# Causal attention on one core: queries and keys in fp32 from SBUF on four 32-partition groups, heads in pairs, with a rewritten opening

## The chip, the cores and the metric

The program runs on one core of one Trainium2 chip. The metric is the device time of one execution in microseconds (us). A smaller time is better.

## What is computed

Four residual steps on x of shape 4 x 512 x 256 (2048 tokens, 16 heads of 16), of which the change touches the first:

```python
x = x + L0_xattn(layernorm(x), ctx_1024)      # causal, relative bias
x = x + L0_ffn(layernorm(x))                  # top 2 of 8 experts, gelu
x = x + L1_xattn(layernorm(x), ctx_1024)      # masked
x = x + L1_ffn(layernorm(x))                  # quantised gate, up, down

# L0_xattn, per batch b and head h (q from x; k and v from ctx_1024)
QEr  = q @ Er.T                               # 512 x 512
Srel = skew(QEr)                              # row i shifted left by 511 - i
attn = softmax(where(causal, (q @ k.T + Srel) / sqrt(16), -inf))
out  = attn @ v
```

## The kernel before

**Stages.** The program is one chain of stages: an opening (the K, V and Q projections of the first layer and its LayerNorm), the causal attention, routing and experts, the masked attention, the closing ffn. The causal attention works through 4 x 16 = 64 heads of a batch, one after the other.

**Opening (`opening`).** SP loads weights, the whole of ctxT (2 MB), the whole of x (2 MB), and the rest. PE makes keys and values half a batch at a time (`PieceProjection.product`, `ValueProjection.product`). ACT copies each 128x512 result twice (fp32, and bf16 as the first piece; L212), DVE splits off two more bf16 pieces (L222, L225, L227) and SP stores them to `packed` in DRAM, 24 transfers for the keys and 24 for the queries (L239). DVE's LayerNorm statistics run in between. The normalising itself is one call for all 16 token tiles, after the last projection of the keys, and PE's transposes (L157) and query projections (L198) wait for that. A head's queries and keys lie in DRAM as six groups of 16 rows, so that one bf16 matmul of 96 rows sums six products of pieces.

**Causal attention (`causal_attention`, L471 to L652).** Only the lower triangle is computed. It is packed in three units a head (CAUSAL_UNITS): the 128 queries of row block 3 with 512 keys; blocks 2 and 0 with 384 and 128; block 1 with 256. A head is 1280 columns (REL_W). `run_heads` runs every engine through steps n. In step n:

- SP loads the queries and keys of head n+8 from `packed` (L400), starts the skewed read of head n+4's relative scores (L515), and the write of head n+6's (L520). The skew is made by writing `stage` to `rel` in DRAM and reading it back with another row pitch, into `bias`.
- PE takes unit by unit: `score` of head n+2 (L541, bf16, and a matmul that adds the mask, L544) into psS, `turn_probs` of head n (four, four and two 128x128 transposes, L555) into psT, `relative` of head n+6 (L533) into psE. At the end of the step comes one `weigh` (L444): the probabilities of four heads by their values, as four fp32 matmuls in four column groups of 32. Each of psE, psS and psT has two banks, used in turn, so that a unit waits for the reader of the unit before the last.
- DVE adds bias and takes the row maximum in one instruction (L603, unit by unit), copies psT to PT (L611) and makes nm = -max/4 (L616). Every four heads it divides by the sums (L464, L466).
- ACT copies psE to `stage` (L643), which has two buffers, so it waits until the write of the head before the last has landed. Between the copies it does head n+1's exponentials in place, with bias nm (L648).
- Pool spreads the values of four heads (L430).

## Time and profile before

| | |
|---|---|
| median of 3 runs | 1235.87 us (1233.3 to 1241.53) |
| the profiled execution | 1240.44 us, span 1238.3 us |
| mean granted clock of TensorE | 0.929 of full speed |
| busy in the span | PE 1011.7, DVE 698.7, ACT 649.7, Pool 199.1 us |
| opening, 0 to 82.1 us | 82.1 us |
| causal attention, 82.1 to 394.2 us | 312.1 us |
| everything behind it | 844.1 us |

The span runs from the first recorded instruction to the last. 2.1 us of the execution lie outside it. The stages are divided by barriers, so their times add up. PE's busy time includes weight loads and moves that other work could cover, so it says nothing of a bound by itself.

### The profile page before, as it was taken

What the parts mean: (1) busy time and instruction counts of PE and PEld (TensorE: products, weight loads), DVE (VectorE), ACT (ScalarE), POOL (GpSimd) and SP (SyncE); (2) the same over time, 40 slices, a digit from 0 to 9 for tenths busy, and PEclk for the clock granted to TensorE, in tenths of its full rate; (3) what the DMA queues carried; (4) which work ended last, traced back from release to release, by engine and by line L of the source; (5) the groups of instructions that cost most, each with busy time, mean ns of one, the idle gap of its engine ahead of it and who ended that gap; (6) DMA issues with size and microseconds to landing.
All of it is one profiled execution on the core that took longest, in us unless ns stands there. A gap on an engine that the chain in (4) does not pass through costs nothing. (4 is left out here: it accounts for less than half of the span.)

```text
span 1238.3 us, 22330 instructions
## 1 busy us (share of the span) xinstructions
PE 1011.7 (82%) x6466; PEld 632.3 (51%) x6467; DVE 698.7 (56%) x2148; ACT 649.7 (52%) x1354; POOL 199.1 (16%) x466
## 2 busy tenths in 40 slices
PE   5746778877888769899999993538999999987487
PEld 3413455444454559898899993212333333334344
DVE  3844778888887541121111110866766666683697
ACT  1345767777773423222233331425777777763687
POOL 0000000000000012233222210002222222240232
PEclk9876999999999979899999997668999999998699
DMA  7478989999983845666666662463111111110001
GB/s 234 149 261 317 332 326 341 342 341 339 339 335 108 315 136 202 220 212 216 215 216 228 221 218 77 131 207 106 46 46 46 48 45 45 46 31 9 1 30 39
DMA packets 91721, 220.29 MB, mean 178 GB/s; under 512 B 8854, under 2 KB 52214, under 8 KB 85654
## 3 DMA queue, kind: packets, MB, share of 16 engines
q1 hardware_dynamic: 87926, 209.46, 49.2%
q0 software_dynamic: 3744, 10.23, 2.2%
q8 instruction: 22, 0.36, 0.1%
q14 instruction: 29, 0.24, 0.1%
HBM read 143.14 MB, written 76.41 MB: 177 GB/s over the span
## 5 line engine op out<-in xcount | busy, mean ns | idle before, releaser
L775 DVE CUSTOM_DVE_ANT_0 unused<-mpsS,mask_bias 128x512 bf16<-128x512 f32 x256 | 172.0, 691 | 84.0 <-PE mpsS L708 83.8
L1482 ACT ACTIVATE hT<-ph,w 128x128 f32<-128x128 f32 x312 | 89.0, 368 | 208.8 <-PE ph L1456 208.8
L802 ACT ACTIVATE mPT<-mpsB 128x512 f32<-128x512 f32 x256 | 152.6, 597 | 81.2 <-PE mpsB L715 74.8
L1456 PE MATMUL ph<-xT,w 128*128 128x128 f32 x1248 | 151.5, 281 | 8.8 <-DMA w<-in_w1p 8.1
L1501 DVE TENSOR_TENSOR xn<-py,b 128x256 f32<-128x256 f32 x39 | 16.5, 424 | 248.7 <-PE py L1466 248.7
L555 PE MATMUL psT<-ident,scores 128*128 128x128 f32 x640 | 108.0, 285 | 57.2 <-ACT scores L648 55.3
L1456 PEld LDWEIGHTS ph<-xT,w 128*128 128x128 f32 x1248 | 146.9, 197 | 11.9 <-issue 10.9
L603 DVE CUSTOM_DVE_ANT_0 scores<-psS,bias 128x512 f32<-128x512 f32 (+3 forms) x256 | 119.7, 487 | 47.8 <-DMA bias<-rel 21.8
L643 ACT COPY stage<-psE 128x512 f32<-128x512 f32 (+1 forms) x192 | 97.5, 510 | 93.6 <-DMA rel<-stage 58.1
L1466 PE MATMUL py<-w,hT 128*128 x624 | 141.2, 379 | 0.7 <-DVE xn L1501 0.7
L648 ACT ACTIVATE scores<-scores,nm 128x128 f32<-128x128 f32 (+3 forms) x256 | 136.6, 565 | 5.2 <-DVE nm L616 5.2
L611 DVE COPY PT<-psT 128x512 f32<-128x512 f32 (+1 forms) x192 | 114.6, 599 | 18.1 <-PE psT L555 17.7
L1466 PEld LDWEIGHTS py<-w,hT 128*128 128x128 f32 x624 | 115.6, 190 | 15.2 <-issue 1.1
L708 PE MATMUL mpsS<-mqk 96*128 96x512 bf16 x256 | 101.2, 397 | 18.7 <-DMA mqk<-packed 14.4
L555 PEld LDWEIGHTS psT<-ident,scores 128*128 128x128 f32 x640 | 68.9, 145 | 80.8 <-ACT scores L648 59.4
L713 PE MATMUL mpsB<-mqk 99*128 99x512 bf16 x256 | 99.0, 387 | 0.1
L715 PE MATMUL mpsB<-maskT,identb 128*128 128x512 bf16 x256 | 98.6, 385 | 0.0
L533 PE MATMUL psE<-ErP,qk 96*128 96x512 bf16 (+3 forms) x256 | 70.8, 322 | 21.1 <-DMA qk<-packed 16.2
L1430 POOL DMA_INDIRECT pair_out<-xn,dst_row x39 | 42.4, 1087 | 214.6 <-DVE xn L1501 214.6
L541 PE MATMUL psS<-qk 96*128 96x512 bf16 (+3 forms) x256 | 73.4, 312 | 1.2 <-DVE mx L603 1.2
L430 POOL TENSOR_TENSOR spreada<-V,zerosa 128x272 f32<-128x272 f32 x16 | 11.5, 719 | 364.7 <-PE psOa L444 281.7
L444 PE MATMUL psOm<-mPT,spreadm 128*32 128x512 f32 x512 | 67.8, 604 | 0.8 <-ACT headsm L451 0.8
(258 smaller groups left out, 1435.8 us busy)
## 6 DMA issues: line engine op xcount, KB each, us to landing
rel<-stage SPq DMA_DIRECT2D x64, 640.0 KB, 6.6
bias<-rel SPq DMA_DIRECT2D x64, 640.0 KB, 7.2
w<-in_w1p SPq DMA_DIRECT2D x39, 1028.0 KB, 5.7
qk<-packed SPq DMA_DIRECT2D x64, 192.0 KB
mqk<-packed SPq DMA_DIRECT2D x64, 192.0 KB
w<-in_w2p SPq DMA_DIRECT2D x8, 1024.0 KB
b<-in_b SPq DMA_DIRECT2D x39, 128.0 KB, 6.1
got<-pair_out SPq DMA_DIRECT2D x8, 512.0 KB, 8.3
```

Source lines behind the costliest of these rows:

```text
L555: tr = nc.tensor.transpose(psT[bank][:, to:to + P], scores[slot][:, at:at + P], ident[:, :])
L603: ttr = nc.vector.tensor_tensor_reduce(out=scores[slot][:, at:at + w], in0=psS[(NU * slot + u) % 2][:, off:off + w], in1=bias[slot][:, at: ...
L611: nc.vector.tensor_copy(PT[r][:, 512 * u:512 * u + WU[u]], psT[(NU * slot + u) % 2][:, 0:WU[u]]).then_inc(s_tev, 1)
L643: nc.scalar.copy(stage[slot % 2][:, 512 * i:512 * i + WU[i]], psE[(NU * slot + i) % 2][:, 0:WU[i]]).then_inc(s_eev, 1)
L648: ex = nc.scalar.activation(scores[slot][:, at:at + w], scores[slot][:, at:at + w], ACT.Exp, bias=nm[:, slot, i:i + 1], scale=1.0 / 4)
L708: nc.tensor.matmul(psS[i % 2][:, :], qk[slot][0:KP, i * P:(i + 1) * P], qk[slot][0:KP, S:2 * S], start=True, stop=True).then_inc(s_smm, 1)
L713: nc.tensor.matmul(psB[i % 2][:, :], qk[slot][:, S + i * P:S + (i + 1) * P], qk[slot][:, 0:S], start=True, stop=False)
L715: nc.tensor.matmul(psB[i % 2][:, :], identb[:, :], maskT[:, i, :], start=False, stop=True).then_inc(s_bmm, 1)
L775: nc.vector.tensor_tensor_reduce(out=unused[:, i, :], in0=psS[i % 2][:, :], in1=mask_bias[:, i, :], scale=1.0, scalar=-3.0e38, op0=ALU.add ...
L802: nc.scalar.activation(PT[r][:, j, :], psB[j % 2][:, :], ACT.Exp, scale=1.0 / 4).then_inc(s_exp, 1)
L1456: mm = nc.tensor.matmul(ph[half][:, q * P:(q + 1) * P], w1[i][:, dk * F + f * P:dk * F + (f + 1) * P], xT[i][:, dk, :], start=(dk == 0), s ...
L1466: mm = nc.tensor.matmul(py[:, 0:D], hT[i][:, f, :], w2[:, bass.ds(e, 1), f * D:(f + 1) * D].rearrange("p a d -> p (a d)"), start=(f == 0), ...
```

## The change

- `packed` is no longer used by this attention. The projections leave fp32 keys in xnT (`kf`) and fp32 queries in the memory of xn (`qf`). The host permutes the heads' rows in the weights, so that heads 0 to 3 of a group of eight lie in the first 16 partitions of the four 32-partition groups and heads 4 to 7 in the second 16. An even-numbered four (`odd` = 0) uses 16 rows. An odd four uses all 32 rows of its group, with queries from ctxT whose other 16 rows DVE has zeroed (`odd` mask, one 128x512 product per batch and half). `er` is Er on all eight 16-row places.
- Heads go in pairs. Pair p lies in row groups 0 and 1 (p even) or 2 and 3 (p odd). In step n PE issues, unit by unit, the scores of pair n+2, the relative scores of pair n+5 (the other two row groups), the mask matmuls (`hide`), and the transposes of pair n. psE, psS and psT are one two-bank tensor each, a bank per head, so that a unit waits for the reader of the unit before it. ACT's psE copies and DVE's psT copies take both heads in one instruction. A step has two `weigh` calls.
- The third `bias` pair lies in x's memory. SP reloads ctxT (2 MB) and x (2 MB) when the last score has been read.
- In the opening, ctxT and x come by batch, LayerNorm runs per batch between the value copies, ACT copies a projection once, and nothing is split or stored.

```diff
+                stage = [sb(ctx, f"stage{r}", [P, 2, REL_W]) for r in range(2)]
+                bias = [sb(ctx, f"bias{r}", [P, 2, REL_W]) for r in range(2)]
+                bias.append(x[:, :, :].rearrange("p t d -> p (t d)")[:, 0:2 * REL_W].rearrange("p (a w) -> p a w", a=2))
...
+                def pair_at(n, ahead):
+                    return n + ahead if 0 <= n + ahead < NP else None
+
+                def piece(p, u, h):
+                    return (NU * p + u) * 2 + h
+
+                def where(p, h):
+                    m = 2 * p + h
+                    b, eh, odd, r = m // HEADS, m % HEADS // ROUND, m % ROUND // GROUP, m % GROUP
+                    return b, eh, odd, slice(ROWS * r, ROWS * r + (ROWS if odd else DH))
+
+                def query(p, h, i):
+                    b, eh, odd, rows = where(p, h)
+                    if odd:
+                        return ctxT[rows, eh, b * S + i * P:b * S + (i + 1) * P]
+                    return qf[rows, b, eh, i * P:(i + 1) * P]
+
...
+                    def read(p):
+                        for h in range(2):
+                            slot = (2 * p + h) % ROUND
+                            sp.wait_ge(s_wr[slot], 16 * (2 * p // ROUND + 1))
...
+                            if p >= len(bias):
+                                sp.wait_ge(s_soft, piece(p - len(bias), NU - 1, h) + 1)
                             skewed = bass.AP(rel[slot].ap().tensor, P - 1, [[REL_W - 1, P], [1, REL_W]])
-                            sp.dma_start(bias[slot][:, :], skewed).then_inc(s_rd[slot], 16)
-                        if h := stage_of(n, r, it, REL):
-                            m, slot, turn = h
...
+                            sp.dma_start(bias[p % len(bias)][:, h, :], skewed).then_inc(s_rd[slot], 16)
+
+                    def write(p):
+                        sp.wait_ge(s_eev, NU * (p + 1))
+                        for h in range(2):
+                            slot = (2 * p + h) % ROUND
+                            wait(sp, s_rd[slot], 16 * (2 * p // ROUND))
+                            sp.dma_start(rel[slot][:, :], stage[p % 2][:, h, :]).then_inc(s_wr[slot], 16)
+
+                    for n in range(-REL, NP - SOFT):
+                        if (p := pair_at(n, READ)) is not None:
+                            read(p)
+                        if (p := pair_at(n, REL)) is not None:
+                            write(p)
+                    for i, name in enumerate(("L1_WkT", "L1_WvT")):
+                        sp.dma_start(wkv[:, i, :, :], a[name].rearrange("(k p) e -> p k e", p=P)).then_inc(s_wkv, 16)
+                    sp.wait_ge(s_soft, 2 * NU * NP)
+                    for half in range(2):
+                        part = slice(half * TOK // 2, (half + 1) * TOK // 2)
+                        sp.dma_start(ctxT[:, :, part], a["ctxT"].rearrange("(k p) t -> p k t", p=P)[:, :, part]).then_inc(s_back, 16)
+                    sp.dma_start(x[:, :, :], a["x"].rearrange("b (i p) d -> p (b i) d", p=P)).then_inc(s_back, 16)
+                    sp.wait_ge(s_wkv, 32)
+                    sp.wait_ge(s_back, 48)
...
+                    def relative(p, u):
...
+                            rows = where(p, h)[3]
+                            for i, off, w in units[u]:
+                                mm = nc.tensor.matmul(psE[:, h, off:off + w], query(p, h, i), er[rows, S - w:S],
+                                                      start=True, stop=True)
                         mm.then_inc(s_emm, 1)
...
+                    def score(p, u):
+                        for h in range(2):
+                            wait(pe, s_soft, piece(p, u, h) - 1)
+                            for at, (i, off, w) in enumerate(units[u]):
+                                nc.tensor.matmul(psS[:, h, off:off + w], query(p, h, i), key(p, h, w),
+                                                 start=(at == 0), stop=False)
+
+                    def hide(p, u):
+                        for h in range(2):
+                            for at, (i, off, w) in enumerate(units[u]):
+                                mm = nc.tensor.matmul(psS[:, h, off + w - P:off + w], identb[:, :], dmask[:, :],
+                                                      start=False, stop=(at == len(units[u]) - 1))
+                            mm.then_inc(s_smm, 1)
+
+                    def turn_probs(p, u):
+                        for h in range(2):
+                            if u == 0:
...
+                            for j, off, w in CAUSAL_KEYS[u]:
+                                for i in range(j, NI):
+                                    at = place[i][0] + j * P
+                                    to = off + (i - j) * P
+                                    tr = nc.tensor.transpose(psT[:, h, to:to + P], scores[p % 3][:, h, at:at + P], ident[:, :])
...
+                    for n in range(-REL, last + 1):
+                        early, soft, late = (pair_at(n, k) for k in (REL, SOFT, 0))
                         for u in range(NU):
-                            if soft:
-                                score(soft[0], soft[1], qk[(r + SOFT) % ROUND], u)
-                            if late:
...
+                            if soft is not None:
+                                score(soft, u)
+                            if early is not None:
+                                relative(early, u)
+                            if soft is not None:
+                                hide(soft, u)
+                            if late is not None:
+                                turn_probs(late, u)
+                        g, half = divmod(n - 2, 2)
+                        if 0 <= g < NBH // GROUP:
+                            for j in (2 * half, 2 * half + 1):
+                                at, w = key_place[j]
+                                vals.weigh(pe, g, g % 2, j, s_tev, NU * 2 * (g + 1),
+                                           lambda h: PT[(2 * g + h // 2) % 4][:, h % 2, at:at + w])
+                        if n % 2 == 0 and 0 <= n // 2 - 2 < NBH // GROUP:
+                            vals.turn(pe, n // 2 - 2, 0)
...
+                                    continue
+                                m = 2 * soft + h
+                                if u == 0:
+                                    dve.wait_ge(s_rd[m % ROUND], 16 * (m // ROUND + 1))
+                                    if soft >= 3:
+                                        dve.wait_ge(s_tmm, NU * (soft - 2))
+                                dve.wait_ge(s_smm, piece(soft, u, h) + 1)
...
+                            if late is not None:
+                                dve.wait_ge(s_tmm, NU * late + u + 1)
+                                nc.vector.tensor_copy(PT[late % 4][:, :, 512 * u:512 * u + WU[u]],
+                                                      psT[:, :, 0:WU[u]]).then_inc(s_tev, 1)
+                            if u == 0 and n % 2 == 1 and 0 <= n // 2 - 2 < NBH // GROUP:
+                                vals.divide(dve, n // 2 - 2, n // 2 % 2)
...
+                        by_row = lambda name: a[name].rearrange("(k p) e -> p k e", p=P)
+                        sp.dma_start(wk[:, :, :], by_row("L0_WkT")).then_inc(s_wk, 16)
+                        for b in range(B):
+                            cols = slice(b * S, (b + 1) * S)
+                            sp.dma_start(ctxT[:, :, cols], a["ctxT"].rearrange("(k p) t -> p k t", p=P)[:, :, cols]).then_inc(s_cx[b], 16)
+                            if b == 0:
+                                sp.dma_start(wv[:, :, :], by_row("L0_WvT")).then_inc(s_wv, 16)
+                                sp.dma_start(bk[:, :], a["L0_bk"]).then_inc(s_wk, 16)
+                                sp.dma_start(bv[:, :], bass.AP(a["L0_bv"].tensor, 0, [[0, P], [1, D]])).then_inc(s_wv, 16)
+                        for b in range(B):
+                            sp.dma_start(x[:, b * NI:(b + 1) * NI, :], a["x"][b].rearrange("(i p) d -> p i d", p=P)).then_inc(s_xb[b], 16)
                         sp.dma_start(ident[:, :], a["ident"]).then_inc(s_const, 16)
-                        q.load(sp)
...
                         ln.turn(pe, 0)
                         for b in range(B):
                             if b + 1 < B:
                                 ln.turn(pe, b + 1)
                             pe.wait_ge(ln.s_ev, DK * (b + 1))
                             for eh in range(DK):
-                                q.product(pe, DK * b + eh)
+                                queries(DK * b + eh)
 
...
+                        for b in range(B):
+                            for t in range(b * NI, (b + 1) * NI):
+                                dve.wait_ge(s_vm, t + 1)
+                                nc.vector.tensor_tensor(V[:, b * HEADS:(b + 1) * HEADS, t % NI, 0:DH],
+                                                        psV[t % 2][:, 0:D].rearrange("p (h d) -> p h d", d=DH),
+                                                        bv[:, :].rearrange("p (h d) -> p h d", d=DH), ALU.add).then_inc(s_vev, 1)
+                                if t % NI == 0:
+                                    dve.wait_ge(s_xb[b], 16)
                                 ln.stats(dve, t)
-                        ln.norm(dve, 0)
-                        dve.wait_ge(s_above, 16)
+                            ln.norm(dve, b)
...
+                        for g in range(B * DK):
+                            b, eh = divmod(g, DK)
+                            dve.wait_ge(s_qev, g + 1)
+                            nc.vector.tensor_scalar(ctxT[:, eh, b * S:(b + 1) * S], qf[:, b, eh, :], odd[:, 0:1], None,
+                                                    ALU.mult).then_inc(s_odd, 1)
```

PE in the middle of the causal attention, before: the step of one head, with `psS` the scores and masks (L541, L544), `psT` the transposed probabilities (L555), `psE` the relative scores (L533).

```order
L541 MATMUL psS<-qk 128x512
L544 MATMUL psS<-dmask,identb 128x128
L555 MATMUL psT<-ident,scores 128x128 x4
L533 MATMUL psE<-ErP,qk 128x512
L541 MATMUL psS<-qk 128x384
L544 MATMUL psS<-dmask,identb 128x128
L541 MATMUL psS<-qk 128x128
L544 MATMUL psS<-dmask,identb 128x128
L555 MATMUL psT<-ident,scores 128x128 x4
L533 MATMUL psE<-ErP,qk 128x384
L533 MATMUL psE<-ErP,qk 128x128
```

After: the first part of the step of one pair, with the scores at L532, relative scores at L524, masks at L538 and transposes at L552.

```order
L532 MATMUL psS<-xnT,ctxT 128x512 x2
L524 MATMUL psE<-er,xn 128x512 x2
L538 MATMUL psS<-dmask,identb 128x128 x2
L552 MATMUL psT<-ident,scores 128x128 x8
L532 MATMUL psS<-xnT,ctxT 128x384
L532 MATMUL psS<-xnT,ctxT 128x128
L532 MATMUL psS<-xnT,ctxT 128x384
L532 MATMUL psS<-xnT,ctxT 128x128
L524 MATMUL psE<-er,xn 128x384
L524 MATMUL psE<-er,xn 128x128
L524 MATMUL psE<-er,xn 128x384
L524 MATMUL psE<-er,xn 128x128
```

Scores and relative scores of two heads now stand directly behind each other, with both heads' masks behind them. Before, a mask and four transposes stood between a score and a relative score.

SP at the start of the causal attention, before: loads of heads (L400), writes (L520) and skewed reads (L515).

```order
L520 DMA rel<-stage 128x1280
L400 DMA qk<-packed 96x1x1024
L520 DMA rel<-stage 128x1280
L400 DMA qk<-packed 96x1x1024
L515 DMA bias<-rel 128x1280
L520 DMA rel<-stage 128x1280
```

After: the same queue, with writes at L500 and reads at L493, two at a time.

```order
L500 DMA rel<-stage 128x1280 x2
L493 DMA bias<-rel 128x1280 x2
L500 DMA rel<-stage 128x1280 x2
L493 DMA bias<-rel 128x1280 x2
L500 DMA rel<-stage 128x1280 x2
L493 DMA x<-rel 128x1280 x2
```

The loads of heads are gone from SP. Each read of a pair now stands directly behind the write of the same pair.

## Rows read from the trace of the kernel before

**Rows 1.** Windows by stage: start:end, length, busy us (instructions) per engine, clock, DMA share, GB/s.

```profile
0.00:82.10 82.10, 51.39 (x160) 29.63 (x161) 49.79 (x126) 27.20 (x43) 0.20 (x4) 0.90 0.67 221
82.10:99.20 17.10, 7.64 (x25) 2.62 (x25) 1.00 (x3) 5.78 (x12) 1.43 (x2) 0.50 0.64 213
99.20:383.30 284.10, 224.87 (x1885) 138.48 (x1884) 230.25 (x787) 205.28 (x447) 10.08 (x14) 0.96 0.89 329
383.30:394.20 10.90, 7.70 (x79) 4.22 (x77) 5.59 (x16) 3.09 (x6) 0.00 (x0) 1.00 0.00 0
394.20:1238.30 844.10, 720.06 (x4322) 457.31 (x4322) 412.09 (x1219) 408.33 (x846) 187.36 (x446) 0.93 0.38 124
```

**Rows 2.** Timeline of PE in the opening: start, length, line, operation, idle before and releaser.

```profile
12.11 3.54 PE L198 MATMUL prpsak<-ctxT,wak 128*128 128x512 f32 x4 [12.11 <-DMA ctxT<-in_ctxT]
...
20.67 3.10 PE L268 MATMUL pvpsa<-wva,ctxT 128*128 128x256 f32 x8 [1.58 <-DVE V L278]
...
44.65 1.99 PE L268 MATMUL pvpsa<-wva,ctxT 128*128 128x256 f32 x8 [0.16 <-DVE V L278]
53.24 3.50 PE L157 MATMUL lnpsa<-ident,xn 128*128 128x128 f32 x16 [6.60 <-DVE xn L131]
...
65.19 7.03 PE L198 MATMUL prpsaq<-xnT,waq 128*128 128x512 f32 x16
86.57 1.03 PE L533 MATMUL psE<-ErP,qk 96*128 96x512 bf16 x3 [14.35 <-DMA qk<-packed]
```

**Rows 3.** Timeline of SP's queue in the opening.

```profile
61.70 17.73 SPq L239 DMA_DIRECT2D packed<-piecesaq  x24
82.09 2.84 SPq L400 DMA_DIRECT2D qk<-packed  x3
```

**Rows 4.** Waits, 200 to 320 us: total us, times, longest.

```profile
ACT stage L643 <- DMA rel<-stage: 30.5, 26, 1.3
...
PE psT L555 <- ACT scores L648: 23.4, 27, 1.4
```

**Rows 5.** DMA, 200 to 320 us: packets, MB, share; then issues, median us to landing.

```profile
q1 hardware_dynamic: 10550, 40.79, 91.0%
...
rel<-stage SPq DMA_DIRECT2D x27, 640.0 KB, 6.7
bias<-rel SPq DMA_DIRECT2D x27, 640.0 KB, 7.2
```

**Rows 6.** Timeline of SP's queue after the last load of a head.

```profile
360.44 0.33 SPq L520 DMA_DIRECT2D rel<-stage  x1
...
364.79 0.32 SPq L520 DMA_DIRECT2D rel<-stage  x1
```

**Rows 7.** Timeline of DVE near the stage's end, with no transfers left.

```profile
373.69 0.69 DVE L603 CUSTOM_DVE_ANT_0 scores<-psS,bias 128x512 f32<-128x512 f32 x1
...
374.30 0.69 DVE L611 COPY PT<-psT 128x512 f32<-128x512 f32 x1
374.90 0.55 DVE L603 CUSTOM_DVE_ANT_0 scores<-psS,bias 128x384 f32<-128x384 f32 x1
...
376.94 0.69 DVE L603 CUSTOM_DVE_ANT_0 scores<-psS,bias 128x512 f32<-128x512 f32 x1
```

**Rows 8.** Timeline of PE around one `weigh`.

```profile
239.60 1.07 PE L444 MATMUL psOa<-PT,spreada 128*32 128x512 f32 x8
240.60 0.39 PE L541 MATMUL psS<-qk 96*128 96x512 bf16 x1
240.83 0.22 PE L544 MATMUL psS<-dmask,identb 128*128 128x128 bf16 x1
```

**Rows 9.** Window of 0.05 us inside that `weigh`, instructions on psOa alone.

```profile
239.65:239.70 0.05, 0.05 (x4) 0.05 (x8) 0.00 (x0) 1.00 0.75 307
```

**Rows 10.** Timeline of PE and DVE: four transposes and their copy.

```profile
241.64 0.66 PE L555 MATMUL psT<-ident,scores 128*128 128x128 f32 x4 [0.59 <-ACT scores L648]
...
242.33 0.69 DVE L611 COPY PT<-psT 128x512 f32<-128x512 f32 x1 [0.23 <-PE psT L555]
```

More of the change, by code:

```diff
@@ L82, in build @@
         s_const = sem("s_const")
-        s_ctx = [sem(f"s_ctx{i}") for i in range(2)]
         class LayerNorm:
@@ L537, in score @@
-                    def score(m, slot, q_k, u):
-                        bank = (NU * slot + u) % 2
-                        wait(pe, s_soft, NU * m + u - 1)
-                        for i, off, w in units[u]:
-                            nc.tensor.matmul(psS[bank][:, off:off + w], q_k[:, i * P:(i + 1) * P],
-                                             q_k[:, S:S + w], start=True, stop=False)
-                            mm = nc.tensor.matmul(psS[bank][:, off + w - P:off + w], identb[:, :], dmask[:, :],
-                                                  start=False, stop=True)
-                        mm.then_inc(s_smm, 1)
@@ L868, in _, with keys @@
-                        pe.wait_ge(s_const, 32)
+                        def keys(g):
+                            b, eh = divmod(g, DK)
+                            wait(pe, s_kev, g - 1)
+                            for dk in range(DK):
+                                mm = nc.tensor.matmul(psK[g % 2][:, :], wk[:, dk, eh * P:(eh + 1) * P], ctxT[:, dk, b * S:(b + 1) * S],
+                                                      start=(dk == 0), stop=(dk == DK - 1))
+                            mm.then_inc(s_km, 1)
@@ new lines, in values, with queries @@
+                        def values(t):
+                            wait(pe, s_vev, t - 1)
+                            for dk in range(DK):
+                                mm = nc.tensor.matmul(psV[t % 2][:, 0:D], ctxT[:, dk, t * P:(t + 1) * P], wv[:, dk, :],
+                                                      start=(dk == 0), stop=(dk == DK - 1))
+                            mm.then_inc(s_vm, 1)
+                        def queries(g):
+                            b, eh = divmod(g, DK)
+                            wait(pe, s_qev, g - 1)
+                            for dk in range(DK):
+                                mm = nc.tensor.matmul(psK[g % 2][:, :], wq[:, dk, eh * P:(eh + 1) * P], xnb[b % 2][:, dk, :],
+                                                      start=(dk == 0), stop=(dk == DK - 1))
+                            mm.then_inc(s_qm, 1)
```

337 lines of the change are left out of this document (121 added, 216 removed).

## The prediction

> **What bounds the kernel now.** I read the windows by stage first [rows 1]. The opening takes 82.1 us, the causal attention 312.1, the rest 844.1. The diff leaves the rest alone, so it enters the sum unchanged.
>
> The opening is a chain on PE with three gaps. PE starts at 12.11, when the first half of ctxT has landed behind 1.8 MB of queue. It idles 6.60 us before 53.24, because the normalising waits for the last key projection [rows 2]. And after its last query product (65.19 + 7.03 = 72.2) it idles 14.35 us, until a head has been stored and loaded again [rows 2]. SP's queue shows the reason: the query stores are issued until 79.4 and the loads start at 82.09 [rows 3].
>
> In the causal attention a head takes 4.35 to 4.48 us (284.1 us for 63.8 heads; two writes are 4.35 apart in [rows 6]). Two things end together there. ACT waits 26 times for the write of `stage`, 30.5 us in all, and PE waits 27 times for the exponentials, 23.4 us [rows 4]. DMA is at 91% [rows 5]. DVE alone would need 3.25 us: with no transfers left, 373.69 to 376.94 is one head [rows 7].
>
> **Part 1: the opening.** By the shapes, 1.0 MB (weights and one batch of ctxT) are ahead of the keys' first product, instead of 1.8 (weights, biases and half of ctxT): PE starts at about 7.5. It then took 34.5 us for keys and values (12.11 to 46.6 [rows 2]), of which about 3.5 us were half clock and one 1.58-us wait. The new order has its own wait, since the statistics of a batch need x, which comes behind all of ctxT. I take 31, so 38.5. Normalising lies between the value copies: for a batch DVE has about 5.5 us of work against PE's 7.3. The 6.60-us gap is gone. Transposes and queries took 53.24 to 72.2, 19.0 us, 1.5 of it at half clock; I take 18, so 56.5. One ACT copy, one DVE product and the barrier follow: **58**. The stores (24 + 24) and their wait are gone, and so is DVE's splitting. Its bounds are 54 and 63. Against 82.1 that is -24.
>
> **Part 2: the load of heads.** 192 KB of 1472 KB per head leave the queues [rows 5]. What does that give? The writes of the last heads have no such loads beside them, and are still 4.35 us apart [rows 6]. So nothing by itself.
>
> **Part 3: the matmuls.** A bf16 score of 512 columns occupied PE for 0.23 us (240.60 to 240.83 [rows 8]). An fp32 matmul of 512 columns takes two passes: 16 records in 7.03 us are 8 matmuls of 0.86 us [rows 2]. One pair has 4 x 1280 columns of scores and relative scores, 8.6 us of PE if nothing runs side by side, and it has only about 8.9 us per pair. So everything hangs on how the row groups run together. The trace has no row groups. Its nearest row is `weigh`: four fp32 matmuls of 512 columns in four column groups, eight records, 1.00 us from 239.60 to 240.60 [rows 8], where four in a row would be 3.44. In 0.05 us at 239.65 four of them run at once [rows 9]. I take 0.90 for four of 512 columns (and for a unit of 384 + 128), 0.48 for four of 256. The other end is 3.44 (one by one).
>
> A rule of the Trainium skill gives another value. "TensorE: Matmul & The Clock Gate", Part 3 (packing small matmuls), reports 3.07 times for four row groups of 32 rows with 512 columns. By it the four would take 3.44 / 3.07 = 1.12, which adds 0.22 twice and 0.12 once per pair, 17 us in all: 1232 instead of 1215. No row here shows row groups.
>
> **Part 4: the new chain.** Each of psE, psS and psT now has one buffer, so PE fills psS only after DVE has read it. Per pair: after DVE's last read of a unit come release 0.13, weight load 0.10, the four matmuls, leaving their mode 0.10, masks 0.06, and latency 0.19 (four transposes at 241.64 were seen by DVE at 242.33, 0.69 for 0.46 of work [rows 10]). That is 0.58 plus the matmuls. DVE's reads of a pair's unit are 2 x 0.61, 2 x 0.69 and 2 x 0.34 [rows 7].
>
> - unit 0 to 1: 1.24 + 1.48 = 2.72
> - unit 1 to 2: 1.40 + 1.06 = 2.46
> - unit 2 to 0 of the next pair: 0.68 + 1.48 + 1.5 = 3.66. The 1.5 are two `weigh` calls (1.79 or 0.95; mean 1.37 from [rows 8] scaled to the columns) and a turn, which now stand ahead of the next scores
> - DVE's divide: 0.16
>
> That makes 9.0 us. DVE's copies (2 x 512 in one, 1.14) lie in the gaps, its busy time is about 6.6. DMA needs 4 x 640 KB at 340 GB/s = 7.7 us, hidden. Two heads took 8.9 before. I take **8.97**: the gain in writes and loads goes into a chain with single buffers.
>
> And ACT's wait for `stage` [rows 4]? A buffer holds a pair and is filled again two pairs later, 17.9 us. Copies of a pair (3 of up to 1024 columns, 3.3) and the landing of two writes (6.7 and 1.9 for the second) fill 11.9 of them. So this wait goes, and the chain above is what is late instead.
>
> **Part 5: both ends.** To the first read of scores: four us of relative scores and copies at half clock, a landed write (6.7), a landed read (7.2) [rows 5], a score: 19, between 15 and 24. It took 17.1 before with 4.5 of load in it. Then 31 periods, 278. Behind them the last pair's reads (4), then the reload of 4.2 MB at the 329 GB/s of [rows 1], 12.8, with 1.5 of latency beside the last exponentials, transposes and divide: 18.5, between 15 and 23. The two weight loads for the second attention stay at nothing: they hide under the same tail.
>
> **Sum.** 58 + 19 + 278 + 18.5 + 844.1 = 1217.6 for the span, with 2.1 outside it 1219.7. The profiled execution was 1240.44 against a median of 1235.87. In proportion: **1215 us**. A measurement of this kernel can tell about 1% (12 us) from no change; 1% faster is 1223.5.
>
> **Rivals.**
>
> - *DMA sets the pace.* A read waits for the write issued just ahead. If each landing then stands behind the other pair's transfers, a period is 4 x 640 KB at 340 GB/s (7.7) plus 1.7 of fixed latency: 9.4, +14 us: 1230. For it: 91% share [rows 5], and the waits of [rows 4]. Against it: 13% of the bytes are gone. Chance 0.13.
> - *Row groups don't run together* (slower). The mechanism: matmuls start in the order of the program, and a second one of the same row group (the 128-column block behind the 384-column one, or the second pass of the same matmul) holds up all behind it. If only the second matmul does so, unit 1 alone suffers: 4 x 0.65 instead of 0.90 + 0.2, +1.5 a pair, +47 us: 1262. If the second pass does so too, four matmuls take five passes of 0.43, 2.15 instead of 0.90, and unit 1 more: +2.8 a pair, +87: 1302. With no overlap at all, about +5 a pair: 1370. It decides against the change from +0.8 us a pair. Against it: the eight records of `weigh` take 1.00 us, not 5 x 0.43 [rows 8], and four run at once [rows 9]. For it: those are column groups with one matmul each. Chance 0.25 (0.12, 0.08, 0.05).
> - *PE's steps are hidden* (faster still). If matmuls start as soon as psS's first bank is free and `weigh` runs beside them, DVE (6.6) or DMA (7.7) sets the pace. A period of 7.6 is -42 us: 1173. For it: PE waited 23.4 of 120 us [rows 4]. Against it: the order of the program on PE. Chance 0.13.
> - *The opening gains nothing*, because x comes too late for the statistics and PE waits there: 1237. Chance 0.02. 2.1 MB of x had landed by 20.67 [rows 2], where the wait for it ended, with less ahead of it now.
>
> The Trainium skill has the order as a rule, in the section named above: matmuls start and end in the order of the program. By it the first case of the second rival holds, and the time is 1262.
>
> **How the numbers follow.** Forecast 0.47: its own range is 1199 to 1232 (opening -4 to +5, the two ends -7 to +9, the period -0.3 to +0.3, not all together). Of it 0.36 are faster by over 1%, 0.10 within, 0.01 slower. DMA: 0.02, 0.09, 0.02. Row groups: 0.00, 0.02, 0.23. Hidden steps: 0.13 faster. Opening: 0.01 within, 0.01 slower. Together 0.51, 0.22, 0.27. The range leaves out the fastest of the hidden case (0.08) and the full hold-up and no overlap (0.12): 1180 to 1275.
>
> **What would show it.** The opening: PE's first product at 7.5, its last near 56, no idle over 2 us. Part 3: four records of psS and psE starting together, 0.9 us per unit 0. Part 4: writes on SP 9.0 apart; DVE waiting for PE's masks (L538) in every unit and hardly for `bias`. The first rival: DVE waits for `bias`, DMA share above 0.9. The second: unit 1's eight matmuls take over 2 us. What makes me wrong: any value of the four matmuls other than 0.90, since it counts three times in each of 31 pairs, or a fill that holds the next pairs up.

## The result and the profile after

The changed kernel takes 1248.24 us (median, 1238.62 to 1262.75) against 1234.96 for the kernel before: a ratio of 1.010, 95% interval 1.0078 to 1.0121. It is 1% slower, where 2% faster was forecast. The ratio leaves out one of its 20 executions, the one at 1262.75. The profiled execution took 1249.16 us, its span is 1247.4.

The windows by stage answer to [rows 1]. The stages are the opening, the way to the first scores, from there to the last scores, the end of the attention, and the rest.

```profile
0.00:55.90 55.90, 46.88 (x160) 28.22 (x161) 26.17 (x98) 18.11 (x30) 0.20 (x4) 1.00 0.30 99
55.90:83.50 27.60, 18.29 (x58) 7.75 (x58) 1.49 (x5) 8.36 (x11) 1.44 (x2) 0.55 0.60 216
83.50:384.20 300.70, 285.28 (x2310) 167.46 (x2314) 210.55 (x658) 197.22 (x349) 9.38 (x13) 0.93 0.74 262
384.20:407.50 23.30, 14.47 (x133) 8.23 (x133) 9.08 (x16) 5.38 (x11) 0.73 (x1) 0.91 0.53 181
407.50:1247.40 839.90, 719.97 (x4322) 458.34 (x4322) 412.22 (x1219) 408.76 (x846) 187.36 (x446) 0.93 0.38 125
```

| us | before | forecast | measured |
|---|---|---|---|
| opening | 82.1 | 58 | 55.9 |
| to the first scores | 17.1 | 19 | 27.6 |
| 31 pairs, and the last one's reads | 295 with the end | 278 + 4 | 300.7 |
| end | (in the line above) | 14.5 | 23.3 |
| rest | 844.1 | 844.1 | 839.9 |

The opening gave 26.2 us. The attention took 351.6 instead of 312.1, which is 39.5 more. The timeline of PE in the opening and at the start of the attention answers to [rows 2]:

```profile
7.27 3.63 PE L856 MATMUL psKa<-ctxT,wka 128*128 128x512 f32 x4 [7.27 <-DMA bka<-in_L_bk]
...
36.56 1.04 PE L156 MATMUL lnpsa<-ident,xn 128*128 128x128 f32 x8
...
48.38 7.03 PE L871 MATMUL psKa<-xnb,wqa 128*128 128x512 f32 x16
56.99 1.13 PE L524 MATMUL psE<-er,xn 16*128 16x512 f32 x4 [1.57 <-PEq L813]
59.22 2.08 PE L524 MATMUL psE<-er,xn 16*128 16x384 f32 x8 [1.10 <-ACT stage L634]
```

PE starts at 7.27, runs without a gap to the transposes at 36.56 and ends at 55.4. Behind that, PE waits for ACT's copy after every unit of relative scores. A unit's matmuls, then their copy, then the next unit's matmuls: that is the single psE. The three pairs ahead of the first scores take 7.3, 8.3 and 8.4 us (from 56.99, 64.33 and 72.63). The clock in that stretch is near 0.5.

The waits and the DMA view from 200 to 320 us answer to [rows 4] and [rows 5]:

```profile
DVE scores L596 <- PE psS L538: 32.5, 19, 2.9
ACT stage L634 <- PE psE L524: 32.2, 26, 3.2
...
PE psT L552 <- DVE PT L603: 2.8, 13, 0.2
```

```profile
q1 hardware_dynamic: 7406, 33.71, 79.4%
...
rel<-stage SPq DMA_DIRECT2D x26, 640.0 KB, 4.1
bias<-rel SPq DMA_DIRECT2D x18, 640.0 KB, 4.6
```

The wait for the write of `stage` is gone, as is PE's wait for the exponentials. DVE and ACT both wait for PE now. PE itself is busy 115.10 of the 120 us in this stretch. DVE waits for the masks 19 times in about 13 pairs: once a pair ahead of unit 0, and now and then ahead of unit 1, not in every unit as forecast. How long is a pair? The timeline of DVE gives it by the first read of each pair:

```profile
204.50 0.69 DVE L596 CUSTOM_DVE_ANT_0 scores<-psS,bias 128x512 f32<-128x512 f32 x1 [2.94 <-PE psS L538]
...
213.13 0.69 DVE L596 CUSTOM_DVE_ANT_0 scores<-psS,x 128x512 f32<-128x512 f32 x1 [1.54 <-PE psS L538]
...
223.13 0.69 DVE L596 CUSTOM_DVE_ANT_0 scores<-psS,bias 128x512 f32<-128x512 f32 x1 [2.94 <-PE psS L538]
```

Pairs take 8.63 and 10.00 us in turn, 9.32 on average. Two heads took 8.9 before. The timeline of PE in one of the long pairs says what fills it:

```profile
211.51 0.70 PE L532 MATMUL psS<-xnT,ctxT 32*128 32x512 f32 x2
211.52 0.70 PE L524 MATMUL psE<-er,xn 16*128 16x512 f32 x2
212.04 0.59 PE L532 MATMUL psS<-xnT,ctxT 32*128 32x512 f32 x2
212.06 0.59 PE L524 MATMUL psE<-er,xn 16*128 16x512 f32 x2
212.58 0.28 PE L538 MATMUL psS<-dmask,identb 128*128 128x128 bf16 x2
...
213.89 1.20 PE L532 MATMUL psS<-xnT,ctxT 32*128 32x384 f32 x3
214.51 0.60 PE L524 MATMUL psE<-er,xn 16*128 16x384 f32 x2
...
215.59 0.40 PE L538 MATMUL psS<-dmask,identb 128*128 128x128 bf16 x4
...
218.72 0.66 PE L552 MATMUL psT<-ident,scores 128*128 128x128 f32 x4 [0.21 <-DVE PT L603]
219.31 1.71 PE L404 MATMUL psOa<-PT,spreada 128*32 128x512 f32 x16
220.95 0.66 PE L417 MATMUL psXa<-ident,headsa 128*128 128x128 f32 x4
221.54 0.70 PE L532 MATMUL psS<-xnT,ctxT 32*128 32x512 f32 x2
```

In unit 0 all four matmuls start within 0.02 us and take 1.07 us to the masks (four in a row would be 3.44). So the row groups do run together. In unit 1 the first head's score starts at 213.89, and the second's with the relative scores 0.62 later, when DVE has read the second head of unit 0. The record of 1.20 us at 213.89 covers that wait, where the matmuls of one head alone are records of about 0.6. So PE's busy time holds waits of this kind. At the end of a pair, `weigh` and the turn take 2.2 us (219.31 to 221.54) on the path to the next scores.

One more thing stands out at the end of the middle stage. The last two pairs take 10.74 and 13.51 us, though PE has no relative scores left for them. The windows of this trace, and of e9 below, which runs the same instructions on PE, show it:

```profile
358.90:375.60 16.70, 16.58 (x82) 8.59 (x80) 8.63 (x27) 6.41 (x14) 0.71 (x1) 0.50 0.14 53
```

```profile
358.00:374.00 16.00, 15.18 (x108) 8.31 (x106) 11.08 (x38) 7.85 (x17) 0.72 (x1) 1.00 0.36 133
```

In the changed kernel's trace the granted clock falls to 0.50 at 358.9 and stays there until 375.6. PE was busy 7.78 of the 8 us before the fall, with no wait for a transfer. In e9 the clock stays at 1.00 and these two pairs take 8.62 and 9.95. The fall costs this execution 5.7 us. What brings it about is open.

### The profile page after: what moved, and what is told of

The parts are those of the page before. It is cut to its first block and busy times, and to the rows that moved or that the text cites. A ratio compares the mean times of both kernels' runs of the same rounds, so it can differ in the third digit from the quotient of the medians.

```text
span 1247.4 us, 21976 instructions
## 1 busy us (share of the span) xinstructions
PE 1084.9 (87%) x6978; PEld 670.0 (54%) x6979; DVE 659.5 (53%) x1993; ACT 637.8 (51%) x1245; POOL 199.1 (16%) x466
## 5 line engine op out<-in xcount | busy, mean ns | idle before, releaser
L634 ACT COPY stage<-psE 128x1024 f32<-128x1024 f32 (+1 forms) x96 | 83.6, 871 | 93.1 <-PE psE L524 90.3
L641 ACT ACTIVATE scores<-scores,nm 128x512 f32<-128x512 f32 (+3 forms) x256 | 125.2, 554 | 7.9 <-DVE nm L609 7.9
L596 DVE CUSTOM_DVE_ANT_0 scores<-psS,bias 128x512 f32<-128x512 f32 (+3 forms) x176 | 77.7, 487 | 88.4 <-PE psS L538 88.1
L603 DVE COPY PT<-psT 128x1024 f32<-128x1024 f32 (+1 forms) x96 | 100.2, 1044 | 9.7 <-PE psT L552 9.6
L552 PE MATMUL psT<-ident,scores 128*128 128x128 f32 x640 | 91.9, 285 | 11.5 <-DVE PT L603 11.3
L552 PEld LDWEIGHTS psT<-ident,scores 128*128 128x128 f32 x640 | 71.5, 145 | 17.9 <-DVE PT L603 17.5
L532 PE MATMUL psS<-xnT,xn 16*128 16x128 f32 (+3 forms) x256 | 73.2, 507 | 6.3 <-DVE mx L596 3.8
L532 PE MATMUL psS<-xnT,ctxT 32*128 32x512 f32 (+3 forms) x256 | 70.1, 496 | 3.1 <-DVE mx L596 0.6
L699 PEld LDWEIGHTS mpsS<-mqk 96*128 96x128 bf16 x256 | 24.9, 98 | 85.9 <-DVE mmx L766 35.2
```

The costliest lines, as they stand in the source:

```text
L532: nc.tensor.matmul(psS[:, h, off:off + w], query(p, h, i), key(p, h, w), start=(at == 0), stop=False)
L552: tr = nc.tensor.transpose(psT[:, h, to:to + P], scores[p % 3][:, h, at:at + P], ident[:, :])
L603: nc.vector.tensor_copy(PT[late % 4][:, :, 512 * u:512 * u + WU[u]], psT[:, :, 0:WU[u]]).then_inc(s_tev, 1)
L641: ex = nc.scalar.activation(to, to, ACT.Exp, bias=nm[:, soft % 3, h, i:i + 1], scale=1.0 / 4)
L699: nc.tensor.matmul(psS[i % 2][:, :], qk[slot][0:KP, i * P:(i + 1) * P], qk[slot][0:KP, S:2 * S], start=True, stop=True).then_inc(s_smm, 1)
```

## The experiments

Theory A at the start: PE's chain in program order sets the period, and both ends of the attention cost what single buffers at half clock cost. The rivals were that PE's order leaves time to win, that fp32 is what costs, or that transfers do.

**e1_relfirst**

```diff
-                            if soft is not None:
-                                score(soft, u)
                             if early is not None:
                                 relative(early, u)
                             if soft is not None:
+                                score(soft, u)
                                 hide(soft, u)
```

> In each unit PE issues the relative scores of pair n+5 ahead of the scores of pair n+2; nothing else is changed. Theory A (the period of 9.3 us per pair is PE's chain in program order, and in units 1 and 2 the relative scores stand 0.6 us behind a score that waits for DVE's read of the second head): the relative scores start beside the first head's, masks end 0.2 us earlier in units 1 and 2, so 8.9 us per pair and about 1236 us. Rival B (PE is simply full: 115 of 120 us busy between 200 and 320 us): the period stays within 0.1 of 9.32 and the time at 1245 to 1250.

1250.06 us, ratio to before 1.010 (1.007 to 1.014), the changed kernel's. The undisturbed pairs take 8.63 and 9.97. So the relative scores behind a waiting score cost nothing, and this part of theory A fell. The size is rival B's, its reason isn't shown: PE's records hold waits, and e3 puts the same instructions into 8.2 us a pair. In this trace the wait for the write of `stage` is back for a while (ACT waits 15.4 us for it between 200 and 320 us), and three pairs of 11.6 to 13.2 us stand among the others.

**e2_apart**

```diff
                             if soft is not None:
                                 score(soft, u)
+                                hide(soft, u)
                             if early is not None:
                                 relative(early, u)
-                            if soft is not None:
-                                hide(soft, u)
```

> Scores, masks, then the relative scores: the masks stand between them, so never more than two row groups run together, but DVE gets its scores sooner. If four groups at once are worth what their records say (1.07 us for four of 512 columns, where two times two would be 2 x 0.9), PE has 1.7 us more per pair and the period goes to about 10.5 to 11, 1285 to 1300 us. Rival: DVE's wait for the scores is the chain and PE has room, the period falls to about 8.8, 1232 us.

1296.06 us, ratio 1.047 (1.043 to 1.051). Pairs take 9.74 and 11.11 in turn, 10.43 on average, which is 1.1 more than with four groups at once. Windows of this kernel show a second loss:

```profile
104.00:154.00 50.00, 50.00 (x198) 26.55 (x196) 19.81 (x60) 18.73 (x33) 0.00 (x0) 0.52 0.49 176
154.00:200.00 46.00, 46.00 (x344) 25.89 (x344) 30.72 (x90) 28.41 (x50) 1.44 (x2) 1.00 0.71 252
```

PE is busy all the time from 104 to 154 us, and the granted clock stays at about half. The three pairs there take 16.4 to 17.9 us.

**e3_weighmid**

```diff
+                            if 0 <= g < NBH // GROUP and u < 2:
+                                for j in (2 * half + u,):
...
+                                    vals.weigh(pe, g, g % 2, j, s_tev, NU * 2 * (g + 1),
...
-                        if 0 <= g < NBH // GROUP:
-                            for j in (2 * half, 2 * half + 1):
```

> The two products of values (weigh) of a step go behind units 0 and 1 instead of both behind unit 2; the turn stays. Theory A (PE's chain has no idle place in units 0 and 1 either): the period stays at 9.2 to 9.4, 1245 to 1250 us. Rival C (weigh lies on the path only because it stands ahead of the next pair's first scores): up to 1.3 us less per pair, 8.0, about 1208 us.

1247.54 us, ratio 1.010 (1.007 to 1.012): the total says that nothing happened. The trace says otherwise. (It is of the fastest of eight executions, 1239.09.) Up to 186 us most pairs take 8.39 and 8.01 in turn, 1.1 less than before the edit: rival C. From there on they take 8 to 12.6. The waits from 186 to 320 us, and the windows, show why:

```profile
ACT stage L634 <- DMA rel<-stage: 40.4, 14, 4.4
```

```profile
110.00:186.00 76.00, 73.70 (x699) 44.78 (x698) 62.53 (x193) 59.24 (x106) 2.88 (x4) 1.00 0.85 295
186.00:320.00 134.00, 126.53 (x1077) 76.71 (x1075) 94.50 (x288) 88.10 (x158) 5.04 (x7) 0.95 0.84 267
```

The wait for `stage` is back, and where PE was held up by it the clock fell (0.68 from 228 to 232). SP's queue has the place:

```profile
126.70 0.80 SPq L500 DMA_DIRECT2D rel<-stage  x2
130.53 1.84 SPq L493 DMA_DIRECT2D bias<-rel  x2
...
176.93 1.87 SPq L493 DMA_DIRECT2D bias<-rel  x2
178.90 1.89 SPq L500 DMA_DIRECT2D rel<-stage  x2
186.63 1.86 SPq L493 DMA_DIRECT2D bias<-rel  x2
188.59 0.87 SPq L500 DMA_DIRECT2D rel<-stage  x2
```

The reads wait for the landing of their own pair's write, and the next write stands behind them. Landing, issue of two reads, issue of two writes, landing: from 176.93 to 186.63 this is 9.7 us. At 126.70 it wasn't so: the write had a gap of over 2 us ahead of it, and the reads could be issued 3.8 us later. With the faster pairs the write comes ever closer behind the reads (151.02 to 156.98 is 6.0, 168.91 to 176.93 is 8.0 us). It then lands later, by the DMA view from 200 to 320 us:

```profile
rel<-stage SPq DMA_DIRECT2D x24, 640.0 KB, 8.4
```

In the changed kernel's view it was 4.1 us.

**e4_bf16**

```diff
-            kf = xnT
+            kf = xnT[:, :, 0:TOK // 2].bitcast(BF16)
+            qodd = ctxT[:, :, 0:TOK // 2].bitcast(BF16)
...
+                        nc.vector.tensor_copy(erb[:, :], er[:, :]).then_inc(s_cc, 1)
```

> Keys, queries and Er are rounded to one bf16 piece, so that each score or relative score is one bf16 pass instead of an fp32 matmul; rows, groups, order and waits stay. This leaves out the exactness of fp32. Theory A (what PE pays for fp32 sets the period and half of the fill): 3 us of matmuls per pair become about 1, the period goes to DVE's or DMA's 7.0 to 7.7, the fill of 27.8 us to about 20, the time to about 1185. Rival D (single buffers and waits for transfers set it): the period stays above 8.8, over 1225 us.

1255.73 us, ratio 1.015 (1.012 to 1.018): slower still, though each score is one bf16 pass now (0.39 us as a record for 512 columns, where fp32 has two of 0.59 to 0.70). Pairs take 7.3 to 13.2 us, 10.1 on average. The first scores come at 72.27. Between 200 and 320 us ACT waits for the write of `stage`, and the clock is low:

```profile
ACT stage L635 <- DMA rel<-stage: 37.7, 12, 4.7
```

```profile
200.00:320.00 120.00, 94.49 (x745) 51.36 (x744) 81.66 (x253) 75.89 (x139) 4.34 (x6) 0.84 0.83 263
```

Rival D by the numbers. So theory E was formed: the order on SP's queue makes a chain of landings of 9 us and more once a write is issued right behind the reads. In the changed kernel's trace the chain isn't closed: between 200 and 320 us SP waits 48.5 us for ACT's copies ahead of the writes, 3.8 us a pair. So the loop of landing and issue needs only some 5.5 us there, as long as reads and writes don't overlap. When PE or the start moves them together, it becomes 9.7 and stays there.

**e5_mid_pool** (first diff, in Pool's block; SP keeps only the writes) and **e6_mid_swap** (second diff), both on top of e3:

```diff
+                    read = reads(pool)
+                    for n in range(-REL, NP):
+                        if (p := pair_at(n, READ)) is not None:
+                            read(p)
```

```diff
-                        if (p := pair_at(n, READ)) is not None:
-                            read(p)
                         if (p := pair_at(n, REL)) is not None:
                             write(p)
+                        if (p := pair_at(n, READ)) is not None:
+                            read(p)
```

> e3's order, and the skewed reads go to Pool's queue, so that SP only writes. In e3 the period was 8.2 us per pair from 113 to 186 us, then 8 to 12.6 while ACT waited 40 us for the writes of stage. Theory E (a write on SP stands behind the reads of the pair before, and these behind the landing of the write before it, so that landings and issues form a chain of 9 us or more): with reads on another queue the period stays at 8.2, about 35 us less than the changed kernel, 1213 us. Rival F (the transfers themselves are too slow at 2.6 MB per pair): the period goes back to 9 to 10 as in e3, 1245 us.

> e3's order, and on SP the write of pair n+5 goes ahead of the reads of pair n+4; both stay on SP. Theory E: a write no longer waits for the landing of the one before, but the reads come one step later, so DVE may wait for bias: 8.2 to 8.8 us per pair, 1215 to 1235 us. Rival F: 9 to 10 per pair, 1245 us.

1215.30 us, ratio 0.983 (0.977 to 0.990), and 1214.24 us, ratio 0.983 (0.978 to 0.988). Two different ways to take the write from behind the reads give the same time. In both the pairs of 8.39 and 8.01 go on to the end. For e6, windows, the waits from 200 to 320 us, and SP's queue:

```profile
200.00:320.00 120.00, 116.83 (x1136) 70.31 (x1138) 99.53 (x306) 94.85 (x169) 5.05 (x7) 1.00 0.88 320
```

```profile
ACT stage L634 <- PE psE L524: 23.5, 29, 1.5
```

```profile
175.90 0.80 SPq L500 DMA_DIRECT2D rel<-stage  x2
176.80 2.16 SPq L493 DMA_DIRECT2D bias<-rel  x2
184.14 0.80 SPq L500 DMA_DIRECT2D rel<-stage  x2
```

No wait for `stage` and none for `bias` is left, at 320 GB/s instead of 267. Theory E is shown, and rival F (too slow a transfer) fell. Unit 1 takes 1.10 us here from the first score to the masks and unit 2 0.65, where DVE has already read both heads.

**e7_ends**

```diff
+                def ps_rel(p, u):
+                    return psT if p < FILL and (NU * p + u) % 2 else psE
+                def ps_turn(p, u):
+                    return psS if p >= NP - SOFT and (NU * p + u) % 2 else psT
...
-                        wait(pe, s_eev, NU * p + u)
+                        wait(pe, s_eev, NU * p + u - (p < FILL))
```

> The changed kernel with two edits at its ends: the relative scores of pairs 0 to 2 alternate between psE and psT (idle then), and the transposes of pairs 30 and 31 between psT and psS. Theory G (both ends are chains of one buffer: product, copy, product): first scores at 75 to 78 us instead of 83.5, and the 22.3 us behind the last scores become 17 to 19; about 1236 us. Rival H (the fill is long because PE runs at half clock there, and the end because of the exponentials): each end gives at most 2 us, 1245 us.

The ends do what theory G says: first scores at 73.74 instead of 83.49, and 17.3 us behind the last ones instead of 23.3, 16 us in all. Yet the time is 1247.59, ratio 1.010 (1.007 to 1.013). The middle lost 11 us of it again: long pairs of up to 11.7 where there were 10.0, and ACT waits 36.3 us for the write of `stage` between 200 and 320 us, where the changed kernel has none. A write takes 8.5 us to land there: it is the chain of e3.

**e8_fullrows**

```diff
                                 relative(early, u)
+                                if early < 3:
+                                    nc.tensor.matmul(psS[:, 0, :], ident[:, :], kf[:, 0, 0:512], start=True, stop=True)
```

> The changed kernel with one extra fp32 matmul of 128 rows and 512 columns behind the relative scores of each unit of pairs 0 to 2 (nine in all), into psS, read by nobody. The granted clock was 0.50 from 60 to 106 us although PE was busy two thirds of that, with matmuls that use 32 or 64 of the 128 rows. Theory I (matmuls on few rows don't raise the clock, those on all rows do): the clock is 1.00 from about 65 us on and the first scores come no later than 83.5 although PE has nine matmuls more. Rival J (the clock follows PE's idle time alone): busier than before, so a little earlier too, but if it stays at 0.50 the first scores come some 5 us later.

One execution, 1258.43 us. Windows of it:

```profile
65.00:75.00 10.00, 10.00 (x20) 3.17 (x21) 0.00 (x0) 2.31 (x3) 0.00 (x0) 0.50 0.73 262
```

PE is busy without a gap from 60 to 90 us, in this window 5.8 of 10 us with matmuls of 128 rows, and the clock stays at 0.50. The first scores come at 91.47, 8 us later. Theory I fell. Rival J named the case of a clock that stays low and 5 us of delay, but idle time can't be what keeps it low here.

**e9_swap**: e6's edit on SP alone.

```diff
-                        if (p := pair_at(n, READ)) is not None:
-                            read(p)
                         if (p := pair_at(n, REL)) is not None:
                             write(p)
+                        if (p := pair_at(n, READ)) is not None:
+                            read(p)
```

> The changed kernel with the write ahead of the reads on SP, and nothing else. Theory A and E together (PE's chain of 9.32 per pair is the longer one, the chain of landings lies just under it): the pairs of 10.0 and 8.63 us go on unchanged, none longer, so 1244 to 1248 us. Rival: the write order alone is worth the 30 us, 1215 us.

1244.05 us, ratio 1.009 (1.005 to 1.013). Pairs of 10.00 and 8.63, and behind the two at half clock none longer. So the two edits of order give 1 and 4 us of the median one by one, and both together 34. With the old place of `weigh` PE sets 9.32 whatever the queue does, and with the old queue the chain of landings sets 9.7 as soon as PE is faster.

**e10_all**: the lines of e3, of e9 and of e7 together.

> e6 (weigh behind units 0 and 1, write ahead of reads) with the two edits of e7 at the ends. In e7 the ends gave 15 us and the middle lost 11, with pairs of 10.4 to 11.7 us. Theory E: those were writes of stage that stood behind reads, and are gone with the new order, so e6's 1214 less 14: 1200 us. Rival: the shorter fill itself sets the transfers against each other, 1210 us or more.

1201.25 us, ratio 0.972 (0.968 to 0.975), 47 less than the changed kernel and 35 less than before. Windows by the same stages as above:

```profile
55.90:74.30 18.40, 16.64 (x58) 9.44 (x58) 1.48 (x4) 8.16 (x11) 1.44 (x2) 0.56 0.55 199
74.30:341.30 267.00, 255.24 (x2322) 153.30 (x2322) 210.35 (x658) 196.69 (x350) 10.12 (x14) 0.95 0.83 304
341.30:358.10 16.80, 12.16 (x117) 7.25 (x118) 8.90 (x17) 4.91 (x10) 0.00 (x0) 1.00 0.73 251
```

The three stages give 9.2, 33.7 and 6.5 us. The ends' gain, in good part given back in e7, is there once the write doesn't stand behind reads.

**e11_bf16_swap**: the lines of e4, of e3 and of e9 together.

> e4 (keys, queries and Er rounded to one bf16 piece, which leaves out the exactness of fp32) with e6's two edits of order. e4 was slower than the changed kernel, at a clock of 0.75 to 0.84 and with 38 us of waiting for stage between 200 and 320 us. Theory E: without that wait the period is DVE's or DMA's, 7.3 to 7.7 us, about 1185 us. Rival K (with bf16 passes PE is idle enough for the clock to fall anyway): the clock stays under 0.95 and the period at 8 or more, 1205 us or more.

1181.65 us, ratio 0.957 (0.953 to 0.962). Pairs take 7.2 to 7.9 us, a few 8.7 to 8.9, and 7.6 on average. The windows:

```profile
100.00:200.00 100.00, 83.50 (x811) 47.31 (x811) 89.55 (x278) 85.03 (x155) 4.32 (x6) 0.98 0.95 352
```

DMA is at 95% and DVE at 90%: in this stretch that is the next floor below the fp32 matmuls. The clock is 0.98 with PE busy 83.5%, where e4 had 0.79 with 78%. So rival K fell, and e4's low clock came with its waits.

**e12_before_opening**: the kernel before, with the order of the opening alone.

```diff
-                    ln = LayerNorm(c1, "a")
+                    ln = LayerNorm(c1, "a", calls=B, on_scalar=True)
...
+                        for b in range(B):
+                            sp.dma_start(x[:, b * NI:(b + 1) * NI, :], a["x"][b].rearrange("(i p) d -> p i d", p=P)).then_inc(s_xb[b], 16)
...
+                            if g % DK == DK - 1:
+                                ln.norm(dve, g // DK)
```

> The kernel before with the new order of the opening alone: ctxT and x by batch, LayerNorm per batch between the value copies (its last step on ACT), Er split last; pieces, stores and the attention stay as before. Theory: the opening's gain of 26 us has two halves, the order (PE's start at 7.3 instead of 12.1, no gap of 6.6, no half clock behind it: 12 to 15) and the stores and loads of heads (the rest). So 1220 to 1223 us. Rival: DVE's splits fill the time that LayerNorm is moved into, and less than 6 us are left, 1229 us.

1242.90 us, ratio 1.006 (1.004 to 1.008): slower. PE starts at 6.52 and then waits for DVE:

```profile
26.84 3.78 PE L269 MATMUL pvpsa<-wva,ctxT 128*128 128x256 f32 x8 [4.36 <-DVE V L279]
...
92.78 1.04 PE L534 MATMUL psE<-ErP,qk 96*128 96x512 bf16 x3 [14.90 <-DMA qk<-packed]
```

The first relative scores come 6 us later than before, at 92.78. After the wait of 4.36 us the eight matmuls take 3.78 us, where the same ones take 1.89 at full clock. Both my theory and the rival, which still saw a gain, promised too much. With DVE's splits in place the new order is worth nothing. A kernel without the splits and in the old order wasn't run, so what each gives of the 26 us isn't shown.

## Why the prediction was wrong

By its own steps:

- **Part 1, the opening**, was right: 55.9 us, 58 forecast. The gap, the splits and the stores went, and x came in time for the statistics. By e12 the order gives nothing while the splits stay.
- **Part 2**, nothing for the loads of heads, is in line with DMA at 79.4% and no wait for transfers in the steady part. No run takes it by itself.
- **Part 3, four matmuls in 0.90 us**: right in kind, too small in size. It was 1.07 for unit 0. Unit 1 took 1.70 and unit 2 1.33 from their first start to the masks, DVE's reading of the second head included, and 1.10 and 0.65 in e6 without it (0.90 and 0.48 forecast). The Trainium skill's 3.07 times ("TensorE: Matmul & The Clock Gate", Part 3, on packing small matmuls), 1.12 us, was the nearer value; the trace has 3.44 / 1.07 = 3.2 times. The row-group rival fell in all three cases: it had at least 2.6 us for unit 1. Matmuls did start in program order, but this didn't hold up the other groups' matmuls for the second pass or the 128-column block. And e2 shows that running four at once is worth 1.1 us a pair.
- **Part 4, the period of 8.97**: measured 9.32. That is 11 us over 31 pairs, a term that was sized too small, just beyond its bounds of 0.3. From one unit's first score to the next PE took 2.4, 3.0 and 3.9 us, where 2.7, 2.5 and 3.8 were forecast. The reason given, single buffers in PE's chain, was half right: with `weigh` moved (e3) and SP's order changed (e6) the same buffers give 8.2. Above that, the two pairs at half clock behind the start took 10.45 each, but the two after them only 8.2 and 8.0, which makes up for it. The last two took 10.7 and 13.5, because of the fall of the clock at 358.9: that is the 5.5 us above 31 times 9.32, and no term of the forecast stood for it.
- **Part 5, both ends**, is the step that failed. "19, between 15 and 24" was 27.6, and "18.5, between 15 and 23", with 4 us of reads in it, was 29.6 (6.3 + 23.3). I added up one pair's way through (products, landing, landing). But PE issues three pairs of relative scores ahead of the first scores, with one psE, and they take 7.3, 8.3 and 8.4 us. At the end I took the reload as the longer way. It had the forecast size (SP's wait for it ends at 398.7, 14.5 us behind the last scores), but PE's and DVE's work for the last pairs, through one psT, ran until 406.2. e7 shows both: with a second buffer 9.8 and 6 us go. How much of what is left of the fill is the half clock, no run separates.
- **"So this wait goes"** (the wait for `stage`, in part 4) held in the profiled execution between 200 and 320 us, but not as safely as argued. I counted a write's landing against two periods. A write is issued only when the reads ahead of it are, and they wait for the landing of the write before. So writes are chained one to one, and in e3, e4 and e7 at 9.7 us and more. This is the first rival, DMA sets the pace: each landing stands behind the other pair's transfers, and its 9.4 is near the size found. What it left out is that the bytes alone don't do it (e6 moves them in 8.2): it takes the order in the queue. In the changed kernel's trace it did not set the pace. In e1, whose pairs are as slow, it did for a while.

The errors by stage, measured less forecast: opening -2, fill +9, middle +19 (11 for the period, 5.5 for the clock's fall at 358.9, 2 for the last reads), end +9, rest -4. Together they are +30, the measured span of 1247.4 less the forecast 1217.6. No run tells what took 4 us from the rest, which the change leaves alone. The wide range, 1180 to 1275, holds the measured 1248, on the side that had a chance of 0.27. That is no merit of the working: the rival that most of this chance was meant for, row groups that don't run together, is not what happened.

What stays open: why the clock stays at half from 58 to 106 us in the changed kernel and to 154 in e2, and why it falls at 358.9. In e8 from 60 to 90 us and in e2 from 104 to 154 PE has no idle time.

## What to carry to other kernels

When a change gives up double buffers, count each end by its whole number of buffer turns (units ahead times product plus copy, at the clock that the stretch will have), not by one element's way through. When a wait disappears, look for the chain that can take its place: here two edits gave 1 and 4 us one by one and 34 us together, and two thirds of the gain at the ends was eaten by the middle until the second chain was cut. In a queue that issues in order, a transfer that waits for its own data's landing must not stand ahead of one that is ready.

## What was not expected of the hardware

- Granted clock at 0.50 with PE busy 100%, for some 50 us in e2 (104 to 154) and 30 in e8 (60 to 90), with fp32 matmuls in row groups, and in e8 with full-array ones between them. In the opening only PE's first four records take 3.63 us, the next four of the same kind 1.88.
- A fall to 0.50 for 16.7 us in the changed kernel's trace, with PE busy 7.78 of the 8 us before it. The same instructions in e9 have a clock of 1.00.
- With the same bf16 matmuls and fewer waits the clock is higher though PE's busy share is not much higher: 0.79 at 78% (e4) and 0.98 at 83.5% (e11), both from 100 to 200 us.
- A write of 640 KB takes 4.1 us to land when it is issued clear of the reads, and 8.4 when it is issued right behind them (e3).
- Four fp32 matmuls of 512 columns in four row groups take 1.07 us, two heads on 16 rows and two on 32 alike.
